# A graph layer in split precision: row sums turned by VectorE and sent through DRAM instead of turned by TensorE

## The chip, the cores and the metric

One core of one Trainium2 chip. The metric is the time of one execution in device microseconds. Three runs of the kernel before took 208.31, 208.48 and 209.1 us; the median is 208.48.

## What is computed

For each of 16 batches, with x of 512 nodes by 128 features and a sparse adjacency matrix adj of 512x512 (all float32):

```
h   = relu(layernorm(x))
HW_r = h @ W_r + c_r            (c_r: a row of 128 numbers, from W_edges and the last 16 rows of W_r), r = 0..6
A   = [adj, adj, shift, adj^T, adj^T, shift^T, identity]
out = x + max over r of (A_r @ HW_r) + b
```

Because A_r @ (h W_r + c_r) = (A_r h) W_r + rowsum(A_r) c_r, the kernel needs two aggregates per batch, g = adj h and gT = adj^T h, the row sums of adj and of its transpose, and seven products with W. (The shift matrices only move nodes around, and the maximum and the products are arranged so that r = 2, 5, 6 use h itself.)

## The kernel before

Everything is held transposed: 128 features on the partitions, 512 nodes along the free dimension. A batch is handled in these steps, and the engines work on neighbouring batches at the same time.

**Split precision.** From batch 2 on (`FIRST = 2`) each operand of a large matmul is split into a part that fits the fast float32r format and the rest: `a_hi` and `a_lo` for adj, `aT_hi` and `aT_lo` for its transpose, `h_hi` and `h_lo`, `hT_hi` and `hT_lo`, and so on. A product then takes three passes (hi·hi, lo·hi, hi·lo) of fast matmuls. adj has 4 chunks of 128 rows. ScalarE makes the hi parts (L414, L423), and as it copies it also adds up each row, which gives `sums`, 128 partitions by 2 directions by 4 chunks. The lo parts of chunks 0 and 1 are made by VectorE (L588, L595), those of chunks 2 and 3 by GpSimd (L330, L337). Batches 0 and 1 aren't split: their aggregates are plain float32 matmuls (L755, L762, L772, L781).

**TensorE, per batch.** `aggregate_T` (L791, L794, L800: 12 matmuls of 128x512), the turning of h (L733: 4 of 128x128), `aggregate` (L809, L811, L817: 12), `turn_sums` (L741: 4 of 128x128), the three products of h (L846, L847, L848: 9), `begin_products` (L836: four matmuls with only 32 rows, which add c_r times the row sum), and the other four products (12). `aggregate` waits until the last maximum of the batch before is taken, because product 6 and g share a PSUM bank. `begin_products` waits for the row sums (`sumsT`) and for `g_lo`.

**The row sums, before.** `part_sums` on GpSimd (L303 twice, L307 twice) writes the sums, split in hi and lo, into a mostly zero tile `sum_parts`; TensorE turns it by four matmuls with an identity (L741); ScalarE copies the result from PSUM into `sumsT` (L465). The rows 0 to 3 of each of four groups of 32 partitions are then used by L836.

**VectorE, per batch b**, in program order: statistics of x for batch b + 2 (L542, L549), `aT_lo` of b (L595), `gT_lo` (L611), `hT_lo` (L606), `rstd` and `shift` of b + 2 (L579, L581), `a_lo` of b + 1 (L588), `h_lo` of b + 1 (L601), `g_lo` of b (L616), then the running maximum `take_best`: two with an added column (L629) and four plain ones (L632), straight from the PSUM banks of the products.

**ScalarE, per batch b:** `a_hi` of b + 1, the standard deviation of b + 2, `gT_hi`, `hT_hi`, h and `h_hi` of b + 1, `g_hi`, the copy into `sumsT`, the first maximum (L472), `aT_hi` of b + 1.

**GpSimd, per batch b:** `finish` of b - 1 (L323, the output sum), then, once `h_lo` of b + 1 is made, the two splits of adj (L330), the DMA that adds x to the bias (L315), the two splits of the transpose (L337), `part_sums` of b + 1.

**Queues.** SP issues nearly all loads and stores, in an order written out by hand; each waits in place until its buffer is free: x of b + 3, adj of b + 2, store of b - 1, bias of b + 1, adjT of b + 2. GpSimd's own queue holds only the accumulating loads of x onto the bias.

There is no planner; each engine's program is the order in which its lines stand, and semaphores alone order the engines among each other.

Of the kernel before, what the change touches and what calls it, by code (L numbers as in the profile page):

```python
# [11 lines left out]
P = 128  # L12
# [14 lines left out]
FIRST = 2  # L27
NX = 4


def gnn_kernel(nc: bass.Bass, x: bass.AP, xT: bass.AP, adj: bass.AP, adjT: bass.AP, W: bass.AP,
               W_rel: bass.AP, W_edges: bass.AP, biasT: bass.AP, outT: bass.AP):
    B, N, F = x.shape
    R, FE, O = W.shape
    REL = FE - F
# [5 lines left out]
    x_dram = x.rearrange("b (c p) f -> b p c f", p=P)  # L41
    adj_dram = adj.rearrange("b (c p) m -> b p c m", p=P)
    adjT_dram = adjT.rearrange("b (c p) n -> b p c n", p=P)
    w_dram = W[:, :F, :].rearrange("r f o -> f r o")

    with ExitStack() as ctx:
# [37 lines left out]
        sumsT = sb("sumsT", [P, N], F32R)  # L84
# [94 lines left out]
        sumsT_ready = sem("sumsT_ready")  # L179
        hT_psum = sem("hT_psum")  # L180
# [31 lines left out]
        def _(sp):  # L212
            def load_x(b):
                q = b % NX
                if b >= NX:
                    sp.wait_ge(h_ready, b - NX + 1)
                    sp.wait_ge(h0_scaled, 1)
                sp.dma_start(x_sb[q][:, :, :], x_dram[b]).then_inc(x_in[q], 16)

            def load_adj(b):  # L220
                q = b % 2
                if b >= 2:
                    if b - 2 < FIRST:
                        sp.wait_ge(sums_ready, 2 * (b - 2) + 1)
                    sp.wait_ge(gT_psum, b - 1)
                if b >= 2 + FIRST:
                    sp.wait_ge(alo_ready, (b - 1 - FIRST) * ND)
                    sp.wait_ge(alo_last_ready, (b - 1 - FIRST) * NG)
                sp.dma_start(adj_sb[q][:, :, :], adj_dram[b]).then_inc(adj_in[q], 16)

            def load_adjT(b):
                q = b % 2
                if b >= 2:
                    if b - 2 < FIRST:
                        sp.wait_ge(sums_ready, 2 * (b - 2) + 2)
                    sp.wait_ge(g_psum, b - 1)
                if b >= 2 + FIRST:
                    sp.wait_ge(aTlo_ready, (b - 1 - FIRST) * ND)
                    sp.wait_ge(aTlo_last_ready, (b - 1 - FIRST) * NG)
                sp.dma_start(adjT_sb[q][:, :, :], adjT_dram[b]).then_inc(adjT_in[q], 16)  # L240
# [11 lines left out]
            sp.dma_start(x_sb[0][:, :HALF, :], x_dram[0][:, :HALF, :]).then_inc(x0_in[0], 16)  # L252
            for c in range(C):
                sp.dma_start(adj_sb[0][:, c, :], adj_dram[0][:, c, :]).then_inc(adj0_in[c], 16)
            sp.dma_start(w_edge[:, :], W_edges).then_inc(wrel_in, 16)
            sp.dma_start(w_rel[:, :], W_rel).then_inc(wrel_in, 16)
            for c in range(C):
                sp.dma_start(adjT_sb[0][:, c, :], adjT_dram[0][:, c, :]).then_inc(adjT0_in[c], 16)
                if c == 0:
                    sp.dma_start(w_sb[:, 0:1, :], w_dram[:, 2:3, :]).then_inc(wh_in, 16)  # L260
                    sp.dma_start(w_sb[:, 1:3, :], w_dram[:, 5:7, :]).then_inc(wh_in, 16)
                    load_x(1)
            sp.dma_start(w_sb[:, 3:5, :], w_dram[:, 3:5, :]).then_inc(wa_in, 16)
            sp.dma_start(w_sb[:, 5:7, :], w_dram[:, 0:2, :]).then_inc(wa_in, 16)
            load_adj(1)
            load_adjT(1)
# [3 lines left out]
            load_adj(2)  # L270
            load_adjT(2)
# [667 lines left out]
```

## Time and profile before

| what | value |
|---|---|
| median of three runs | 208.48 us |
| the profiled execution | 208.36 us |
| its span, from the first to the last instruction | 206.6 us |
| TensorE busy | 198.2 us, 96% |
| VectorE busy | 178.8 us, 87% |
| ScalarE busy | 162.3 us, 79% |
| GpSimd busy | 130.0 us, 63% |
| granted TensorE clock, mean | 1.000 |
| DMA: bytes moved, mean rate | 51.07 MB, 247 GB/s |
| packets in all / under 8 KB | 33747 / 33728 |

A busy share is the share of the span in which the engine works on something. Matmuls overlap in the pipeline, so a busy TensorE is not one at its peak; how long a group of matmuls holds the engine is read from the starts, or from the chain of waits. That chain is followed back from the last instruction: at each step to the operation that released it, or to the one before it on its engine. An operation of VectorE that doesn't wait for the one before it starts some 0.08 us before that one's recorded end.

### The profile page before, as it was taken

Reading aid. Unit: us, or ns where it says so; the run is one execution under the profiler, and the core shown is the slowest. Engines: PE = TensorE matmul, PEld = TensorE weight load, DVE = VectorE, ACT = ScalarE, POOL = GpSimd, SP = SyncE. Lnnn points to the kernel's source line nnn. Section 1 sums busy time; section 2 is a strip of 40 time slices with the busy share of each in tenths; the row PEclk is TensorE's granted clock in tenths of the full one; section 3 lists DMA queues with packets and bytes.
Section 4 is the critical chain, followed back from the end, with each engine's and each line's share of the span. In section 5 each row is a group of like instructions: output and inputs, shape, how many; then the busy total and the mean of one; then the engine's idle time right before and its main releaser. Section 6 shows DMA issues by size and latency. Waiting matters only on the chain.

```text
span 206.6 us, 3426 instructions
## 1 busy us (share of the span) xinstructions
PE 198.2 (96%) x922; PEld 152.2 (74%) x922; DVE 178.8 (87%) x411; ACT 162.3 (79%) x432; POOL 130.0 (63%) x166
## 2 busy tenths in 40 slices
PE   6999999799999999999999999999999999999991
PEld 6556468568788787878878787877878786887871
DVE  3587869999889998999889998999989999997565
ACT  3987989597979969696997969698896969685230
POOL 4140246969593977939594696919695486959600
PEclk9999999999999999999999999999999999999999
DMA  6999999987896959699795969779695969923201
GB/s 183 311 360 361 361 359 270 304 268 224 312 293 187 387 127 392 153 336 263 244 351 140 389 126 368 218 257 342 210 352 100 396 136 295 261 91 47 65 2 51
DMA packets 33747, 51.07 MB, mean 247 GB/s; under 512 B 1872, under 2 KB 11328, under 8 KB 33728
## 3 DMA queue, kind: packets, MB, share of 16 engines
q1 hardware_dynamic: 31152, 46.53, 66.2%
q0 software_dynamic: 2304, 4.20, 13.1%
q10 hardware_dynamic: 272, 0.13, 0.2%
q8 instruction: 7, 0.11, 0.2%
q14 instruction: 12, 0.10, 0.2%
HBM read 46.65 MB, written 4.19 MB: 246 GB/s over the span
## 4 chain that ended last, share of the span: by engine, by line
PE 70%; DMA 11%; DVE 6%; SPq 4%; POOL 3%; issue 3%; ACT 0%; DVEq 0%; ACTq 0%; POOLq 0%
PE bank_p L846 10%; PE bank_p L847 8%; PE bank_p L848 8%; DMA x_bias<-in_biasT_dram 8%; PE bank_g L809 5%; PE bank_g L811 5%; PE bank_g L817 5%; PE bank_gT L800 5%; PE bank_gT L794 5%; PE bank_gT L791 5%; DMA x_bias<-in_xT_dram 4%; PE bank_p L836 3%; PE bank_p L733 3%; PE bank_p L741 2%; DVE best L632 2%
## 5 line engine op out<-in xcount | busy, mean ns | idle before, releaser
L330 POOL TENSOR_TENSOR a_lo<-adj_sb,a_hi 128x512 fp32r<-128x512 f32 x28 | 36.1, 1310 | 38.0 <-DVE h_lo L601 36.9
L337 POOL TENSOR_TENSOR aT_lo<-adjT_sb,aT_hi 128x512 fp32r<-128x512 f32 x28 | 39.5, 1575 | 0.0
L632 DVE TENSOR_TENSOR best<-bank_p,best 128x512 f32<-128x512 f32 x48 | 33.2, 691 | 5.8 <-PE bank_p L848 4.7
L414 ACT ACTIVATE a_hi<-adj_sb 128x512 fp32r<-128x512 f32 x56 | 34.5, 620 | 0.0
L423 ACT ACTIVATE aT_hi<-adjT_sb 128x512 fp32r<-128x512 f32 x56 | 34.4, 620 | 0.0
L629 DVE SCALAR_TENSOR_TENSOR best<-bank_p,c_col,best 128x512 f32<-128x512 f32 x32 | 23.9, 748 | 5.0 <-ACT best L472 4.4
L595 DVE TENSOR_TENSOR aT_lo<-adjT_sb,aT_hi 128x512 fp32r<-128x512 f32 x28 | 25.4, 945 | 0.0
L435 ACT ACTIVATE h<-x_sb,shift,rstd 128x128 f32<-128x128 f32 x60 | 24.6, 488 | 0.0
L323 POOL TENSOR_TENSOR o_sb<-best,x_bias 128x512 f32<-128x512 f32 x15 | 20.8, 1384 | 3.4 <-DMA x_bias<-in_xT_dram 3.4
L846 PE MATMUL bank_p<-hT_hi,w_hi 128*128 128x512 f32 x48 | 20.1, 420 | 0.4 <-ACT sumsT L465 0.4
L588 DVE TENSOR_TENSOR a_lo<-adj_sb,a_hi 128x512 fp32r<-128x512 f32 x28 | 20.3, 765 | 0.0
L315 POOL DMA_DIRECT2D x_bias<-in_xT_dram x16 | 13.9, 868 | 9.2 <-DMA x_bias<-in_biasT_dram 9.2
L847 PE MATMUL bank_p<-hT_hi,w_lo 128*128 128x512 f32 x48 | 18.7, 390 | 0.0
L848 PE MATMUL bank_p<-hT_lo,w_hi 128*128 128x512 f32 x48 | 18.7, 389 | 0.0
L809 PE MATMUL bank_g<-aT_hi,h_hi 128*128 128x512 f32 x56 | 16.5, 416 | 1.5 <-DVE best L632 1.5
L387 ACT ACTIVATE std<-mean_var,eps 128x4 f32<-128x4 f32 x15 | 4.4, 296 | 16.7 <-DVE mean_var L549 16.7
L453 ACT ACTIVATE gT_hi<-bank_gT 128x512 fp32r<-128x512 f32 x16 | 9.5, 596 | 10.2 <-PE bank_gT L800 10.2
L303 POOL CAST sum_parts<-sums 128x16 fp32r<-128x16 f32 x32 | 14.8, 710 | 2.2 <-ACT summed L403 2.2
L817 PE MATMUL bank_g<-aT_lo,h_hi 128*128 128x512 f32 x56 | 15.3, 392 | 0.0
L811 PE MATMUL bank_g<-aT_hi,h_lo 128*128 128x512 f32 x56 | 15.1, 391 | 0.0
L800 PE MATMUL bank_gT<-a_lo,h_hi 128*128 128x512 f32 x56 | 15.0, 390 | 0.0
L791 PE MATMUL bank_gT<-a_hi,h_hi 128*128 128x512 f32 x56 | 15.0, 389 | 0.0
(118 smaller groups left out, 493.9 us busy)
## 6 DMA issues: line engine op xcount, KB each, us to landing
adj_sb<-in_adj_dram SPq DMA_DIRECT2D x15, 1024.0 KB, 5.5
adjT_sb<-in_adjT_dram SPq DMA_DIRECT2D x15, 1024.0 KB, 7.1
x_bias<-in_biasT_dram SPq DMA_DIRECT2D x16, 256.0 KB, 4.8
x_bias<-in_xT_dram POOLq DMA_DIRECT2D x16, 256.0 KB, 5.1
x_sb<-in_x_dram SPq DMA_DIRECT2D x15, 256.0 KB, 7.9
out_dram<-o_sb SPq DMA_DIRECT2D x15, 256.0 KB, 4.1
adj_sb<-in_adj_dram SPq DMA_DIRECT2D x4, 256.0 KB, 4.4
adjT_sb<-in_adjT_dram SPq DMA_DIRECT2D x4, 256.0 KB, 4.8
```

The source lines that it names most:

```text
L330: nc.gpsimd.tensor_tensor(a_lo[q][:, c, :], adj_sb[q][:, c, :], a_hi[q][:, c, :].bitcast(F32), ALU.subtract).then_inc(alo_last_ready, 1)
L337: nc.gpsimd.tensor_tensor(aT_lo[q][:, c, :], adjT_sb[q][:, c, :], aT_hi[q][:, c, :].bitcast(F32), ALU.subtract).then_inc(aTlo_last_ready, 1)
L414: nc.scalar.activation(a_hi[q][:, c, :], adj_sb[q][:, c, :], ACT.Copy, accum_out=sums[q][:, 0, c:c + 1]).then_inc(ahi_ready, 1)
L423: nc.scalar.activation(aT_hi[q][:, c, :], adjT_sb[q][:, c, :], ACT.Copy, accum_out=sums[q][:, 1, c:c + 1]).then_inc(aThi_ready, 1)
L595: nc.vector.tensor_tensor(aT_lo[q][:, c, :], adjT_sb[q][:, c, :], aT_hi[q][:, c, :].bitcast(F32), ALU.subtract).then_inc(aTlo_ready, 1)
L632: op = nc.vector.tensor_tensor(best[q][:, :], product, best[q][:, :], ALU.max)
L809: nc.tensor.matmul(bank_g[:, 0:N], h_hi[q][:, c, :], aT_hi[q][:, c, :], start=(c == 0), stop=False)
L811: nc.tensor.matmul(bank_g[:, 0:N], h_lo[q][:, c, :], aT_hi[q][:, c, :], start=False, stop=False)
L817: last = nc.tensor.matmul(bank_g[:, 0:N], h_hi[q][:, c, :], aT_lo[q][:, c, :], start=False, stop=(c == C - 1))
L846: nc.tensor.matmul(dst, w_hi[:, i, :], hi[:, nodes], start=start, stop=False)
L847: nc.tensor.matmul(dst, w_lo[:, i, :], hi[:, nodes], start=False, stop=False)
L848: return nc.tensor.matmul(dst, w_hi[:, i, :], lo[:, nodes], start=False, stop=stop)
```

## The change

1. **Row sums from batch 2 on (`TURNED = 2`).** GpSimd's `part_sums`, TensorE's L741 and ScalarE's L465 stay for batches 0 and 1 only. For the others VectorE copies the sums into a tile of 32 columns (hi), subtracts to get the lo columns, and transposes this tile in blocks of 32x32. SP stores the result to a scratch array in DRAM (128 runs of 128 bytes), waits for that, and issues four loads, each of which fills four partitions of `sumsT` with rows of 2 KB. `sumsT` becomes a pair. L836 waits for these loads.
2. **Place of the new work.** In VectorE's program it stands behind the third of the six maxima of the batch before.
3. **Batch 2 half whole.** Chunks 2 and 3 of its two aggregates are plain float32 matmuls; chunks 0 and 1 are still split. GpSimd no longer splits anything of batch 2.
4. **GpSimd's order.** `finish` waits for `aT_lo`, the splits for `a_lo` and `h_lo`; all four splits follow each other, and the DMA that adds x comes behind them.
5. **Queues.** adj and adjT from batch 3 on are loaded from ScalarE's queue, behind `hT_hi` and behind the first maximum; the standard deviation moves behind `hT_hi`.
6. **Layouts.** x, adj, adjT and W are laid out in DRAM by partitions, so that what a partition receives is one run.

```diff
+            def turn_blocks(b):
+                q = b % 2
+                i = b - TURNED + 1
+                s = sums[q][:, :, :].unsqueeze(2).to_broadcast([P, 2, 2, C])
+                dve.wait_ge(ahi_ready, (b - FIRST + 1) * NS)
+                dve.wait_ge(aThi_ready, (b - FIRST + 1) * NS)
+                nc.vector.tensor_copy(sum_cols[:, :, :, 0, :], s).then_inc(cols_hi, 1)
+                dve.wait_ge(cols_hi, i)
+                nc.vector.tensor_tensor(sum_cols[:, :, :, 1, :], s, sum_cols[:, :, :, 0, :].bitcast(F32),
+                                        ALU.subtract).then_inc(cols_lo, 1)
+                dve.wait_ge(cols_lo, i)
+                if i >= 2:
+                    dve.wait_ge(scratch_in, 16 * (i - 1))
+                nc.vector.transpose(sum_blocks[:, :], sum_cols[:, :, :, :, :].rearrange("p d k s c -> p (d k s c)")
+                                    .bitcast(F32)).then_inc(blocks_turned, 1)
...
                 for i in range(1, NPROD - int(b == B - 1)):
+                    if i == NH + 1 and b + 1 < B:
+                        turn_blocks(b + 1)
                     take_best(b, i)
...
+    scratch_blocks = scratch.rearrange("d r (c j s) -> j (d r c) s", c=C, s=GROUP)
+    scratch_rows = scratch.rearrange("d r n -> r d n").unsqueeze(2).to_broadcast([4, 2, 2, N])
...
+            def turn_sums(b):
+                i = b - TURNED + 1
+                q = b % 2
+                sp.wait_ge(blocks_turned, i)
+                sp.dma_start(scratch_blocks, sum_blocks[:, :]).then_inc(scratch_in, 16)
+                sp.wait_ge(scratch_in, 16 * i)
+                sp.wait_ge(prod_psum, (b - 1) * NPROD)
+                for r in range(4):
+                    sp.dma_start(sumsT[q][r:P:GROUP, :].bitcast(F32), scratch_rows[r]).then_inc(sumsT_in[q], 16)
...
             for b in range(1, B):
+                if b >= TURNED:
+                    turn_sums(b)
                 if b + 3 < B:
                     load_x(b + 3)
-                if b + 2 < B:
-                    load_adj(b + 2)
                 store(b - 1)
                 if b + 1 < B:
                     load_bias(b + 1)
-                if b + 2 < B:
-                    load_adjT(b + 2)
...
-            for b in range(1, B):
-                if b >= 2:
-                    finish(b - 1)
+            add_bias(2)
+            for b in range(2, B):
+                pool.wait_ge(aTlo_ready, (b - FIRST + 1) * ND)
+                finish(b - 1)
                 if b + 1 < B:
+                    pool.wait_ge(alo_ready, (b - FIRST + 2) * ND)
                     pool.wait_ge(hlo_ready, b - FIRST + 2)
                     split_adj_last(b + 1)
+                    split_adjT_last(b + 1)
                     add_bias(b + 1)
-                    split_adjT_last(b + 1)
-                    part_sums(b + 1)
...
+                split_gT(b)
+                split_hT(b)
                 if 2 <= b < B - 2:
                     std_of(b + 2)
-                split_gT(b)
-                split_hT(b)
+                if b + 2 < B:
+                    load_adj(b + 2)
                 if b + 1 < B:
                     make_h(b + 1)
                 split_g(b)
-                copy_sumsT(b)
+                if b < TURNED:
+                    copy_sumsT(b)
                 begin_best(b)
+                if b + 2 < B:
+                    load_adjT(b + 2)
...
+                if b == FIRST:
+                    pe.wait_ge(adj_in[q], times(b))
+                    for c in range(ND, C):
+                        nc.tensor.matmul(bank_gT[:, 0:N], h[q][:, c, :], adj_sb[q][:, c, :],
+                                         start=(c == ND), stop=False)
...
+                if b < TURNED:
+                    pe.wait_ge(sumsT_ready, b + 1)
+                else:
+                    pe.wait_ge(sumsT_in[b % 2], 64 * (b // 2))
...
-                turn_sums(b)
+                if b < TURNED:
+                    turn_sums(b)
```

## Rows read from the trace of the kernel before

**Rows 1.** Busy time by stretch, one batch: start:end, us, then busy us (x instructions).
```profile
115.17:127.00 11.83, 11.81 (x58) 9.36 (x58) 11.05 (x27) 10.09 (x28) 9.56 (x11) 1.00 0.87 278
```

**Rows 2.** The chain of waits (start us, us, what): L836 of batches 2 and 15, one batch between.
```profile
44.60 0.50 PE bank_p L836 x3
...
119.09 0.91 PE bank_gT L791 x4
...
125.02 0.39 PE bank_p L741 x4
125.41 0.29 PE bank_p L846
125.70 0.23 PE bank_p L847
...
127.51 0.43 PE bank_p L836 x3
...
130.94 0.91 PE bank_gT L791 x4
...
198.97 0.44 PE bank_p L836 x2
```

**Rows 3.** The timeline of VectorE and GpSimd, 111 to 128 us (start us, us, ...).
```profile
112.92 0.16 DVE L581 SCALAR_TENSOR_TENSOR shift<-mean_var,rstd 128x4 f32<-128x4 f32 x1
...
117.14 2.14 DVE L632 TENSOR_TENSOR best<-bank_p,best 128x512 f32<-128x512 f32 x3 [0.21 <-PE bank_p L848]
...
118.41 2.84 POOL L337 TENSOR_TENSOR aT_lo<-adjT_sb,aT_hi 128x512 fp32r<-128x512 f32 x2
...
121.12 1.29 DVE L595 TENSOR_TENSOR aT_lo<-adjT_sb,aT_hi 128x512 fp32r<-128x512 f32 x2
...
122.48 0.69 DVE L611 TENSOR_TENSOR gT_lo<-bank_gT,gT_hi 128x512 fp32r<-128x512 f32 x1
...
122.94 1.30 POOL L323 TENSOR_TENSOR o_sb<-best,x_bias 128x512 f32<-128x512 f32 x1
...
123.69 0.17 DVE L579 RECIPROCAL rstd<-std 128x4 f32<-128x4 f32 x1
123.89 0.37 DVE L581 SCALAR_TENSOR_TENSOR shift<-mean_var,rstd 128x4 f32<-128x4 f32 x1
...
125.38 0.68 DVE L601 TENSOR_TENSOR h_lo<-h,h_hi 128x512 fp32r<-128x512 f32 x1
...
126.14 2.54 POOL L330 TENSOR_TENSOR a_lo<-adj_sb,a_hi 128x512 fp32r<-128x512 f32 x2 [1.90 <-DVE h_lo L601]
...
126.95 1.54 DVE L629 SCALAR_TENSOR_TENSOR best<-bank_p,c_col,best 128x512 f32<-128x512 f32 x2 [0.29 <-ACT best L472]
```

**Rows 4.** The timeline at three meetings of VectorE and GpSimd.
```profile
13.40 0.74 POOL L360 TENSOR_TENSOR w_lo<-w_sb,w_hi 128x256 fp32r<-128x256 f32 x1 [2.98 <-DVE w_hi L665]
13.44 0.72 DVE L581 SCALAR_TENSOR_TENSOR shift<-mean_var,rstd 128x4 f32<-128x4 f32 x1
...
14.86 0.86 DVE L675 TENSOR_SCALAR c_low<-c_rest,row_lo 128x128 f32<-128x128 f32 x1
14.90 0.73 POOL L364 TENSOR_TENSOR w_lo<-w_sb,w_hi 128x256 fp32r<-128x256 f32 x1
...
31.23 1.28 POOL L330 TENSOR_TENSOR a_lo<-adj_sb,a_hi 128x512 fp32r<-128x512 f32 x1 [1.14 <-ACT a_hi L414]
31.28 1.79 DVE L588 TENSOR_TENSOR a_lo<-adj_sb,a_hi 128x512 fp32r<-128x512 f32 x1
```

**Rows 5.** DMA issues: what, queue, count, KB each, median us from issue to landing.
```profile
out_dram<-o_sb SPq DMA_DIRECT2D x15, 256.0 KB, 4.1
...
out_dram<-o_sb SPq DMA_DIRECT2D x2, 128.0 KB, 1.7
...
w_edge<-in_W_edges_dram SPq DMA_DIRECT2D x1, 0.4 KB, 3.5
```

**Rows 6.** The timeline of ScalarE's queue at its one load.
```profile
0.80 0.47 ACTq L475 DMA_DIRECT2D x_sb<-in_x_dram  x1
```

**Rows 7.** The timeline of TensorE: an unsplit aggregate, and aggregate of batch 2.
```profile
23.71 3.67 PE L781 MATMUL bank_g<-adjT_sb,h 128*128 128x512 f32 x8
...
37.89 1.19 PE L809 MATMUL bank_g<-aT_hi,h_hi 128*128 128x512 f32 x4 [1.45 <-DVE best L632]
```

More of the change, by code:

```diff
@@ L83, in gnn_kernel @@
         sum_parts = pair("sum_parts", [P, C, 2, 2, GROUP], F32R)
-        sumsT = sb("sumsT", [P, N], F32R)
+        sumsT = pair("sumsT", [P, N], F32R)
+        sum_cols = sb("sum_cols", [P, 2, 2, 2, C], F32R)
+        sum_blocks = sb("sum_blocks", [P, GROUP])
         x_bias = pair("x_bias", [P, N])
@@ L179, in gnn_kernel @@
         sumsT_ready = sem("sumsT_ready")
+        cols_hi = sem("cols_hi")
+        cols_lo = sem("cols_lo")
+        blocks_turned = sem("blocks_turned")
+        scratch_in = sem("scratch_in")
+        sumsT_in = [sem(f"sumsT_in{i}") for i in range(2)]
         hT_psum = sem("hT_psum")
@@ L697, in _ @@
                 take_best(1, i)
+            turn_blocks(2)
             for b in range(2, B):
@@ L783, in aggregate_whole, with split_chunks @@
                 last.then_inc(g_psum, 1)
+            def split_chunks(b):
+                return range(ND if b == FIRST else C)
             def aggregate_T(b):
@@ L806, in aggregate @@
                 pe.wait_ge(best_done, b * NBEST)
-                for c in range(C):
+                if b == FIRST:
+                    pe.wait_ge(adjT_in[q], times(b))
+                    for c in range(ND, C):
+                        nc.tensor.matmul(bank_g[:, 0:N], h[q][:, c, :], adjT_sb[q][:, c, :],
+                                         start=(c == ND), stop=False)
+                for c in split_chunks(b):
                     pe.wait_ge(aThi_ready, (b - FIRST) * NS + c + 1)
-                    nc.tensor.matmul(bank_g[:, 0:N], h_hi[q][:, c, :], aT_hi[q][:, c, :], start=(c == 0), stop=False)
-                for c in range(C):
+                    nc.tensor.matmul(bank_g[:, 0:N], h_hi[q][:, c, :], aT_hi[q][:, c, :],
+                                     start=(c == 0 and b > FIRST), stop=False)
+                for c in split_chunks(b):
                     nc.tensor.matmul(bank_g[:, 0:N], h_lo[q][:, c, :], aT_hi[q][:, c, :], start=False, stop=False)
-                for c in range(C):
+                for c in split_chunks(b):
                     if c < ND:
@@ L830, in begin_products, with add_sums @@
                     for nodes, to in zip(HALVES, last_banks):
-                        add_sums(NPROD - 1, to, nodes, start=True)
-            def add_sums(i, to, nodes=slice(0, N), start=False, stop=False):
+                        add_sums(b, NPROD - 1, to, nodes, start=True)
+            def add_sums(b, i, to, nodes=slice(0, N), start=False, stop=False):
                 group = ORDER_A.index(ORDER[i])
                 rows = slice(group * GROUP, (group + 1) * GROUP)
-                return nc.tensor.matmul(to[:, nodes], c_rows[rows, :], sumsT[rows, nodes], start=start, stop=stop)
+                return nc.tensor.matmul(to[:, nodes], c_rows[rows, :], sumsT[b % 2][rows, nodes], start=start, stop=stop)
             def passes(i, dst, nodes=slice(0, N), start=False, stop=False):
@@ L919, with by_partition @@
     batch, nodes, features = x.shape
+    chunks = nodes // P
+    def by_partition(a):
+        return np.ascontiguousarray(np.transpose(a.reshape(batch, chunks, P, a.shape[2]), (0, 2, 1, 3)))
     given = {
-        "x": np.ascontiguousarray(x),
+        "x": by_partition(x),
         "xT": np.ascontiguousarray(np.transpose(x, (0, 2, 1))),
-        "adj": np.ascontiguousarray(adj),
-        "adjT": np.ascontiguousarray(np.transpose(adj, (0, 2, 1))),
-        "W": np.ascontiguousarray(L0_gnn_W),
+        "adj": by_partition(adj),
+        "adjT": by_partition(np.transpose(adj, (0, 2, 1))),
+        "W": np.ascontiguousarray(np.transpose(L0_gnn_W[list(ORDER), :features, :], (1, 0, 2))),
         "W_rel": np.ascontiguousarray(L0_gnn_W[:, features:, :]).reshape(-1, L0_gnn_W.shape[2]),
```

127 lines of the change are left out of this document (62 added, 65 removed).

## Prediction

> **What bounds the kernel now.** I began with busy time by stretch, one stretch per batch: in a steady batch of 11.83 us TensorE is busy for 11.81, VectorE 11.05, ScalarE 10.09, GpSimd 9.56, at a granted clock of 1.00, which is the 2.4 GHz level [rows 1]. Two engines are nearly full, so I read the chain of waits next. From L836 of batch 2 at 44.60 to L836 of batch 15 at 198.97 the chain lies almost wholly on TensorE [rows 2]: 154.4 us for 13 batches, 11.87 each. TensorE paces the kernel. One batch runs from 119.09 to 130.94, 11.85 us, of which the turning of the row sums (L741) holds 0.39, and the first matmul behind it needs 0.29 where the ones that follow need 0.23 [rows 2].
>
> Then VectorE's timeline, because the change gives it work. Its three maxima start at 117.14, and 0.29 us before 126.95 it has finished everything up to the next batch's first two maxima: 9.52 us [rows 3]. With those two (1.54) and the join it needs 11.0 a batch. In that stand two waits that are not work: the shift took 0.37 instead of 0.16, and gT_lo started some 0.15 late behind aT_lo (122.48, though aT_lo was over at 122.41 and two such operations otherwise overlap by 0.08) [rows 3]. Bare VectorE work is **10.7 us a batch**, against TensorE's 11.85.
>
> Last I looked for operations that took longer than their like. VectorE's split of 128x512 needs 0.68 (two in 1.29 [rows 3]), but took 1.79 when GpSimd had begun its own split 0.05 us earlier; the shift of 128x4 took 0.72 when a GpSimd subtract had begun 0.04 earlier, and ended as that one ended; a VectorE operation with one tensor input (c_low) took 0.86 beside a GpSimd subtract of 0.73 [rows 4]. So a VectorE operation that reads two SBUF tensors stands still until a GpSimd operation in progress ends, however small it is. This decides the case.
>
> **The change part by part.** *TensorE.* L741 goes from batch 2 on: 0.39, and 0.06 of the slow first matmul, so 0.45 a batch; 11.85 becomes 11.4. Nothing else of its steady work changes.
>
> *VectorE.* Each batch gains a copy of 16 elements, a subtract of 16 and a block transpose of 32, each waiting for the one before. The nearest row is the reciprocal and the shift that waits for it: starts 0.20 apart [rows 3]. Three make 0.6; the transpose isn't in the trace, so 0.45 (ends of 0.15 each, the bare duration) to 0.8 (a transpose twice as long). 10.7 + 0.6 = 11.3, just under the new 11.4: **no slack is left**, and any wait of VectorE above 0.1 us a batch is paid in full. In return the finish now waits for aT_lo, so GpSimd's output sum runs beside gT_lo and hT_lo, which read PSUM; that takes away the waits named above, which I have already left out of the 10.7.
>
> *Where the new operations fall.* GpSimd starts its splits of the next batch 0.08 after h_lo ends (126.06, 126.14), two in 2.54 [rows 3]. Until now the bias DMA stood between them and the two splits of aT; it is moved behind, so the first aT split follows at about 2.6 after h_lo, the second at about 3.85, the end at about 5.1 (1.25 to 1.4 each, from two in 2.84 [rows 3]). VectorE reaches turn_blocks after g_lo (0.6), two maxima (1.54) and the third (0.71): about 2.75 after h_lo. That is in the middle of those splits. If VectorE came later it would not escape: turn_blocks waits for the last aT_hi of ScalarE, and GpSimd's splits need these same operands, so they start when it does or shortly before. The subtract reads two SBUF tensors; by rows 4 it waits for the split in progress. The copy comes within 0.15 us of the start of the first split and can be just before or just behind it.
>
> I take **one wait of about 1.05 us** a batch (most of one split of 1.25, as the subtract asks 0.2 after the split began). Ends: 0.3, when it meets a split at its end, and 1.4, a whole long one. So VectorE sets the pace: 10.7 + 0.6 + 1.05 = 12.35 us a batch, 0.5 slower than now, and TensorE waits for the maxima, g_lo and hT_lo.
>
> *The way through DRAM.* The blocks go out in 128-byte runs, the queue's engine waits, then four loads are issued. The trace shows no such transfer. Nearest: a load of 0.4 KB in pieces of 4 bytes landed after 3.5 us in a full stretch, 128 KB at the quiet end after 1.7 [rows 5]; four issues at 0.47 each, ScalarE's row [rows 6]. So 1.7 + 1.7 + 1.9 = 5.3 to 3.5 + 3.5 + 1.9 = 8.9; I take 7. What covers it: from the turned blocks (third maximum over at 117.85, plus 0.6) to L836 of the next batch (127.51 less 0.45) are 8.6 us [rows 2, 3]. Cost nothing; if the cover is gone, the excess is paid per batch. By the Trainium skill ("DMA: Bandwidth & Descriptors", "Anatomy of one DMA — SWDGE (gpsimd) path") a transfer costs about 2.0 us fixed, most of it the receipt; its fit is for GpSimd's queue. By that the way would take an estimated 5.9 and batch 2 would not wait for it at all; the row of 3.5 is longer, and the measurement counts.
>
> *Batch 2 (half whole).* GpSimd splits nothing of it, so VectorE's a_lo at 31.28 no longer meets it: two splits at 1.79 become 1.29, the maxima of batch 1 end 2.2 us sooner, and TensorE's wait of 1.45 at 37.89 goes [rows 7]. L741 goes too (0.45). Against that four chunks run in full precision: eight such matmuls, four chunks, took 3.67 [rows 7], 0.9 a chunk, against three passes at 0.23; 0.2 each, +0.8. L836 of batch 2 would come at 44.60 - 1.1 = 43.5. But its sums start only when batch 1's maxima are over, about 37.89 - 2.2 = 35.7, and need 0.6 and the way through DRAM: 41.6 to 45.2. I take 44.0.
>
> *The rest.* ScalarE loses a copy of 0.6 and issues two DMAs at 0.47 [rows 6]: +0.3, 10.4 a batch, hidden behind 11.4 and more; its waits before these loads are all met by work it has just waited for. Without that cover the aT_hi splits, and turn_blocks, come 0.3 later. SP now waits for the blocks ahead of an x load, a store and a bias load. These blocks are turned in the batch before, ahead of the finish for which the store already waits, and x has three batches of lead: nothing. GpSimd loses the four small operations for the sums and sits idle in their place. The layout by partitions makes runs longer; in the first 33 us TensorE waits for chunks of adj, but eight matmuls there take hardly longer than the 3.67 of batch 1 [rows 7]: nothing, between 0 and -1 us.
>
> **The sum.** To L836 of batch 2: 44.0. Twelve batches at 12.35: 148.2. The one before the last has no statistics (about 1.2 less on VectorE), so TensorE's 11.4. From L836 of batch 15 to the end 206.6 - 198.97 = 7.6 [rows 2]. Outside the span the profiled execution spends 208.36 - 206.6 = 1.8. Together 213.0 against 208.36; the median of the runs is 208.48, 0.1 above it. **Forecast 213.0**, slower by 2.2%. Its own range, with 0.45 to 0.8 for the work and 0.3 to 1.4 for the wait, and 43.5 to 45 for batch 2: 202 (never below TensorE's 11.4) to 220, most of it 207 to 217.
>
> **Rivals.** *No collision (faster).* If these operations are too short to be held, or GpSimd is off the port when they come, TensorE stays the bound: 44.0 + 13 x 11.4 + 7.6 + 1.8 = 201.6. The place is turn_blocks, the price is the wait there, and it decides below 0.7 us a batch: at a period of 12.0 the sum is 208.8. For it: a reciprocal beside GpSimd's output sum (122.94 to 124.24) took 0.17 [rows 3]. Against it: the shift, smaller still, waited.
>
> *Two waits.* If the copy too is held, it waits for the first split and the subtract for the second, as GpSimd takes its next operation in between: 2.15 us instead of 1.05, 13.45 a batch: 44.0 + 12 x 13.45 + 11.95 + 7.6 + 1.8 = 226.7. For it: c_low with one tensor input waited [rows 4]. Against it: the copy may come first, and no plain copy beside GpSimd is in the trace. The Trainium skill ("SBUF — State Buffer", "Who interferes with whom") has copies, casts and tensor_scalar in their two-port modes take the pair shared with GpSimd, and whoever is first holds it for the whole instruction; by that rule this is the outcome unless the copy is first, and c_low's 0.86 agrees with it.
>
> *The way through DRAM is late.* If each leg takes 4.1, as stores of 256 KB in mid-run do [rows 5], it needs 10.1 instead of 8.6, and TensorE waits 1.5 us a batch at L836 whatever VectorE does: 44.0 + 13 x 12.9 + 9.4 = 221. Against it: these transfers are 16 KB, and no load stands ahead of them in their queue.
>
> **How the numbers follow.** Chances: one wait 0.37, no collision 0.33, two waits 0.22, late sums 0.08. The range reaches from no collision less 1.5 for the layout and a good batch 2, 200.0, to 224.0, which leaves out most of the two-wait case. A measurement of this kernel tells 0.5%, about 1 us. Faster: no collision and the low end of one wait, 0.36; within 0.5%: 0.06; slower 0.58.
>
> **What would show it.** Right: L741 gone from batch 2 on; in the steady part VectorE without idle time, its subtract in turn_blocks at 1 us or more and ending when a GpSimd aT split ends, TensorE idle at L836 or L846 with VectorE as releaser, a period near 12.35. A subtract of 0.2 and TensorE unbroken at 11.4 would make it wrong towards faster; copy and subtract both above 1 us towards 227; TensorE waiting at L836 for sumsT's loads would show the late sums.

## The result and the profile after

The changed kernel takes **226.53 us** (median of four runs, 224.19 to 227.72) against 208.39 us for the kernel before on the same chip: a ratio of 1.083, with a 95% interval of 1.075 to 1.092. (The ratio leaves out the run of 227.72, which lies more than 1.5% above the fastest; with it the medians alone give 1.087.) It is 18 us slower; the forecast was 213.0, and its range ended at 224.0. The profiled execution took 225.96, with a span of 224.2.

Busy time by engine, and the granted clock in 40 slices of the span, from the page of the kernel after:

```profile
PE 201.0 (90%) x862; PEld 146.9 (66%) x862; DVE 189.5 (85%) x453; ACT 155.6 (69%) x418; POOL 104.2 (46%) x106
...
PEclk9999999958999999999999999999996999999998
```

No engine is full any more. TensorE is busy for nearly as long as before, but its 201.0 now holds stretches at a lower clock, and the span is 18 us longer.

From its waits (engine, line, what was waited for: us in all, times, longest):

```profile
PEld bank_p L897 <- DMA sumsT<-scratch_dram: 18.7, 12, 3.1
DVE best L671 <- PE bank_p L909: 14.8, 15, 3.5
PE bank_p L897 <- DMA sumsT<-scratch_dram: 13.1, 9, 2.7
```

TensorE waits at L897 (L836 before) for the row sums in most batches, and VectorE waits 14.8 us for product 3, which follows L897. The chain of waits through one batch, L897 at 100.52 to L897 at 114.35, as far as it runs through the sums (start us, us, what):

```profile
102.64 0.29 DVE sum_cols L648
...
102.96 1.23 DVE sum_cols L650
...
104.21 0.22 DVE sum_blocks L655
...
104.45 2.00 DMA scratch_dram<-sum_blocks
...
106.47 0.51 SPq L237
...
108.06 6.25 DMA sumsT<-scratch_dram
...
114.35 0.50 PE bank_p L897 x3
```

Where TensorE's own work stood in the chain of before [rows 2], there is now the store to DRAM (2.00), three issues (1.6 with their gaps), and the fourth load from its issue until all four have landed (6.25). The same turning in VectorE's and GpSimd's timeline, with the first turning of the kernel, at 36.79, ahead of it:

```profile
36.79 0.16 DVE L648 CAST sum_cols<-sums 128x16 fp32r<-128x16 f32 x1
36.98 0.18 DVE L650 TENSOR_TENSOR sum_cols<-sums,sum_cols 128x16 fp32r<-128x16 f32 x1
37.20 0.21 DVE L655 STREAM_TRANSPOSE sum_blocks<-sum_cols 128x32 f32<-128x32 f32 x1
...
101.60 2.54 POOL L328 TENSOR_TENSOR aT_lo<-adjT_sb,aT_hi 128x512 fp32r<-128x512 f32 x2
...
102.64 0.28 DVE L648 CAST sum_cols<-sums 128x16 fp32r<-128x16 f32 x1
...
102.96 1.22 DVE L650 TENSOR_TENSOR sum_cols<-sums,sum_cols 128x16 fp32r<-128x16 f32 x1
```

At 36.79 no GpSimd operation runs beside them, and copy and subtract take 0.16 and 0.18. In the steady part (batches 4 to 15) the subtract took 1.21 to 1.23 in nine batches of twelve and 0.18 in three, the copy 0.25 to 1.29: on average the two waited **1.38 us** a batch.

From here on the **period** is the distance between the starts of that first matmul of `begin_products` in batches 2 and 15, over 13: 11.87 before, **13.11** after. It splits in two without a rest: 4.11 from L897 to the issue of the next batch's store, and 9.00 from that issue to the next L897, "the way" below. The way is not all DRAM: the four loads had landed 8.4 us after the store's issue on average (5.5 to 9.9), and in batches 3, 8 and 12 they had landed 0.5 to 5.0 us before TensorE came to L897. In the profiled executions the difference of 17.6 us is 1.5 for batch 2 (L897 at 46.06 for L836 at 44.60 [rows 2]), 13 x 1.24 = 16.1 for the period, and next to nothing in the tail. Two of the 13 batches are long without late sums of their own: the one from 46.06 took 14.25 and the one from 166.74 took 12.95, at granted clocks of 0.78 and 0.87.

### The profile page after: what moved, and what is told of

The parts are those of the page before. It is cut to its first block, busy times and chain, and to the rows that moved or that the text cites. A ratio compares the mean times of both kernels' runs of the same rounds, so it can differ in the third digit from the quotient of the medians.

```text
span 224.2 us, 3374 instructions
## 1 busy us (share of the span) xinstructions
PE 201.0 (90%) x862; PEld 146.9 (66%) x862; DVE 189.5 (85%) x453; ACT 155.6 (69%) x418; POOL 104.2 (46%) x106
## 3 DMA queue, kind: packets, MB, share of 16 engines
q0 software_dynamic: 2304, 4.20, 12.9%
HBM read 47.11 MB, written 4.42 MB: 230 GB/s over the span
## 4 chain that ended last, share of the span: by engine, by line
DMA 32%; PE 30%; DVE 17%; SPq 8%; ACT 6%; issue 6%; ACTq 1%; DVEq 0%
DMA sumsT<-scratch_dram 16%; DMA scratch_dram<-sum_blocks 10%; SPq L237 5%; PE bank_p L907 5%; DVE sum_cols L650 4%; PE bank_p L909 4%; PE bank_p L908 4%; DVE sum_cols L648 3%; DMA adj_sb<-in_adj_dram 3%; DMA w_sb<-in_W_dram 3%; PE bank_p L897 3%; DVE best L671 3%; ACT a_hi L410 2%; ACT aT_hi L419 2%; PE bank_gT L842 2%
## 5 line engine op out<-in xcount | busy, mean ns | idle before, releaser
L321 POOL TENSOR_TENSOR a_lo<-adj_sb,a_hi 128x512 fp32r<-128x512 f32 x26 | 32.9, 1285 | 27.8 <-DVE a_lo L611 27.8
L671 DVE TENSOR_TENSOR best<-bank_p,best 128x512 f32<-128x512 f32 x48 | 32.6, 680 | 15.5 <-PE bank_p L909 14.8
L314 POOL TENSOR_TENSOR o_sb<-best,x_bias 128x512 f32<-128x512 f32 x15 | 19.2, 1283 | 38.4 <-DVE aT_lo L618 35.9
L328 POOL TENSOR_TENSOR aT_lo<-adjT_sb,aT_hi 128x512 fp32r<-128x512 f32 x26 | 33.1, 1297 | 0.0
L897 PE MATMUL bank_p<-sumsT,c_rows 32*128 32x512 f32 (+1 forms) x49 | 8.3, 505 | 13.7 <-DMA sumsT<-scratch_dram 13.1
L611 DVE TENSOR_TENSOR a_lo<-adj_sb,a_hi 128x512 fp32r<-128x512 f32 x28 | 18.1, 688 | 0.0
L618 DVE TENSOR_TENSOR aT_lo<-adjT_sb,aT_hi 128x512 fp32r<-128x512 f32 x28 | 17.7, 673 | 0.0
L897 PEld LDWEIGHTS bank_p<-sumsT,c_rows 32*128 32x128 f32 x49 | 3.3, 188 | 20.1 <-DMA sumsT<-scratch_dram 18.7
L875 PE MATMUL bank_g<-aT_lo,h_hi 128*128 128x512 f32 x54 | 15.8, 401 | 0.1
L907 PE MATMUL bank_p<-gT_hi,w_hi 128*128 128x512 f32 x32 | 14.7, 459 | 0.0
```

The source lines that it names most:

```text
L314: nc.gpsimd.tensor_tensor(o_sb[q][:, :], best[q][:, :], x_bias[q][:, :], ALU.add).then_inc(out_ready, 1)
L321: nc.gpsimd.tensor_tensor(a_lo[q][:, c, :], adj_sb[q][:, c, :], a_hi[q][:, c, :].bitcast(F32), ALU.subtract).then_inc(alo_last_ready, 1)
L328: nc.gpsimd.tensor_tensor(aT_lo[q][:, c, :], adjT_sb[q][:, c, :], aT_hi[q][:, c, :].bitcast(F32), ALU.subtract).then_inc(aTlo_last_ready, 1)
L671: op = nc.vector.tensor_tensor(best[q][:, :], product, best[q][:, :], ALU.max)
L907: nc.tensor.matmul(dst, w_hi[:, i, :], hi[:, nodes], start=start, stop=False)
```

## The experiments

The theory to begin with: a closed loop. L897, product 3, the third maximum, the turning with its waits for GpSimd, the store and the loads, and L897 of the next batch follow one another, so both delays are paid in series. Rival A: the port waits alone cost the time. Rival B: the late sums alone do.

**1. GpSimd out of the way.** GpSimd's aT splits wait for the turned blocks:

```diff
             def split_adjT_last(b):
+                pool.wait_ge(blocks_turned, b - TURNED + 1)
```

> GpSimd starts its two splits of aT of a batch only once that batch's blocks are turned, so the copy and the subtract of the row sums meet no GpSimd operation and should take 0.16 and 0.18 us, as they do in the changed kernel where GpSimd rests. Theory (a closed loop: product 3, its maximum, the turning, the way through DRAM, begin_products of the next batch): the loop loses about 1.35 us a batch (copy 0.76, subtract 0.93 on average) but keeps the 9.2 us of the way through DRAM: period 11.9 instead of 13.1, time about 210 (208 to 213), and TensorE still waits for the row sums in every batch. Rival A (the port waits alone cost the time, VectorE sets the pace): period 11.4, time 202. Rival B (the late sums alone cost it, the port waits only fill idle time of VectorE): unchanged, 224 to 227.

Measured: 222.09 us, period 12.64; copy and subtract 0.16 to 0.18 in every batch. The part from L897 to the store fell from 4.11 to 3.02, but the way grew from 9.00 to 9.62. The transfers themselves did not: the sums landed 8.3 us after the store's issue on average, as before, but spread from 6.6 to 11.5. All three forecasts, the theory's and both rivals', missed. Busy time by stretch, in batches of three kinds (us, then PE, PEld, DVE, ACT, POOL busy, the clock, DMA share, GB/s):

```profile
48.29:62.52 14.23, 14.23 (x54) 10.95 (x55) 9.91 (x27) 5.11 (x13) 5.42 (x5) 0.78 0.48 141
...
101.17:112.53 11.36, 11.36 (x54) 8.95 (x54) 10.56 (x29) 9.45 (x28) 7.20 (x7) 1.00 0.76 242
136.55:150.31 13.76, 11.40 (x54) 8.95 (x53) 13.05 (x30) 11.77 (x34) 8.80 (x8) 0.99 0.89 288
```

Where the sums landed in less than 8.6 and the clock was full, the batch ran at TensorE's own 11.36, and 2.77 + 8.6 is just that; what lands sooner gains nothing. In four batches like the third line they landed after 9.9 to 11.5 and the excess was paid in full, 9.2 of the 16.6 us that the 13 batches took beyond 11.36 each. The other 7.4 are in four batches like the first line (12.8 to 14.2): their own sums had landed after 6.6 to 7.0, but each stands behind a batch whose sums TensorE had awaited for 2.4 to 5.0 us, and TensorE ran them at a clock of 0.78 or 0.87.

**2. The way through DRAM out of the loop.** `begin_products` takes the sums of the batch before, from three buffers (so the output lacks its own batch's sums; the store also waits for the loads of the batch before):

```diff
-                q = b % 2
+                q = b % 3
...
-                    pe.wait_ge(sumsT_in[b % 2], 64 * (b // 2))
+                    pe.wait_ge(sumsT_in[(b - 1) % 3], 64 * ((b - 3) // 3 + 1))
```

> Here begin_products adds the row sums of the batch before instead of its own, from the same stores and loads into three buffers: the way through DRAM has a whole batch more and cannot delay TensorE, while the copy and the subtract can still meet GpSimd's splits. The output then holds the wrong batch's row sums. Theory (loop): without the way through DRAM the port waits alone are left, VectorE's 10.7 + 0.6 + about 1.35 = 12.65 us a batch: period 12.3 to 12.8, batch 2 no longer waits (begin_products near 43.5 instead of 46.1), time 211 to 220. Rival A (the port waits alone cost the time): period unchanged at 13.1, time 222 to 226. Rival B (the late sums alone): TensorE is the bound again, period 11.4, time about 202.

Measured: 221.87 us, period 12.93 (13.13 in the steady batches), and no wait for sums. This misses the theory's range on the high side and lies by rival A's. One batch in VectorE's and GpSimd's timeline:

```profile
109.28 2.54 POOL L327 TENSOR_TENSOR a_lo<-adj_sb,a_hi 128x512 fp32r<-128x512 f32 x2 [2.05 <-DVE a_lo L618]
...
111.77 2.55 POOL L334 TENSOR_TENSOR aT_lo<-adjT_sb,aT_hi 128x512 fp32r<-128x512 f32 x2
...
112.00 1.10 DVE L655 CAST sum_cols<-sums 128x16 fp32r<-128x16 f32 x1
...
113.14 1.21 DVE L657 TENSOR_TENSOR sum_cols<-sums,sum_cols 128x16 fp32r<-128x16 f32 x1
```

The copy waits for one split and the subtract for the next, in 12 of the 14 turnings: two waits, 1.97 us. By the page, the chain is now mostly VectorE's:

```profile
DVE 62%; PE 16%; issue 12%; DMA 3%; ACT 3%; SPq 2%; DVEq 0%; ACTq 0%
```

Each cause alone keeps the kernel near 222. So there are **two bounds at nearly the same height**: the loop (13.11 a batch as changed, 12.64 with the port free, both with some batches at a lower clock) and VectorE held at the port (13.13). Taking one away uncovers the other.

**3. Both edits together.**

> Both edits of the two runs before together: no GpSimd split beside the turning, and the row sums of the batch before in begin_products (the output holds the wrong batch's row sums). Theory: nothing is left but TensorE's own work, 11.4 us a batch, and VectorE's 11.3 beside it: about 43.5 + 13 x 11.4 + 7.7 + 1.8 = 201 (200 to 204). If a third thing costs time as well (the adj loads that are now issued late, or VectorE's 11.3 not fitting into 11.4), it is seen here alone: 205 or more.

Measured: 206.35 us, period 11.74. Of the 20 us, the two single edits gave 4 and 5. (These are single runs, and the kernel after itself ranged over 3.5 us.) The rest over 201 is the third thing that was allowed for: five of the 13 batches took 11.9 to 12.9, the others 11.3 to 11.5. In one of the long ones the timeline shows VectorE's a_lo beside GpSimd's output sum, 2.67 for the two splits instead of 1.28; in the other four it is the small `shift` that stands still beside the same sum, 0.86 to 1.87 instead of 0.17:

```profile
87.78 0.86 POOL L312 DMA_DIRECT2D x_bias<-in_xT_dram  x1 [3.09 <-DMA x_bias<-in_biasT_dram]
...
87.86 2.67 DVE L619 TENSOR_TENSOR a_lo<-adj_sb,a_hi 128x512 fp32r<-128x512 f32 x2
...
88.39 1.58 POOL L320 TENSOR_TENSOR o_sb<-best,x_bias 128x512 f32<-128x512 f32 x1
```

**4. The rest of the change alone.** TensorE turns all row sums again:

```diff
-TURNED = 2
+TURNED = 16
...
                     split_adjT_last(b + 1)
+                    part_sums(b + 1)
                     add_bias(b + 1)
...
-            turn_blocks(2)
...
-                    if i == NH + 1 and b + 1 < B:
-                        turn_blocks(b + 1)
```

> The changed kernel with the row sums of all batches turned as before the change: small operations of GpSimd, four matmuls of TensorE, a copy by ScalarE. Half of the third batch in full precision, the order of GpSimd, the queues and the layouts stay as changed. Theory: all of the loss lies in the turning, so this runs at the period before, 11.85, or slightly under it, and gains the 1.1 us of batch 2: 207 (204 to 209). Rival C (the queues, GpSimd's order or the layouts cost something too): above 210.

> The changed kernel with TensorE turning the row sums of all batches, once more, now timed against the kernel before in several rounds. One look gave 205.8 with batch 2's begin_products 1.9 us earlier and a period of 11.81 instead of 11.87. Theory: 205.5 to 206.5, a ratio near 0.988. Rival (that difference was the chance of one look): a ratio of 0.995 to 1.005.

Measured: 205.8 in a single run; in the repetition a median of 206.55 (12 runs) against 208.81 (17 runs), ratio **0.989**, interval 0.986 to 0.993. The other parts together are a gain of about 1%, and this version beats both kernels. In the single run `begin_products` of batch 2 stands at 42.74 (43.34 in the repetition, 44.60 before), the period is 11.81, and the page has the chain on TensorE again:

```profile
PE 96%; DVE 2%; issue 0%; POOL 0%; DVEq 0%; POOLq 0%
```

**5. Another place for the turning.** One maximum earlier, ahead of that of product 3; without and with GpSimd's splits held until the blocks are turned:

```diff
-                    if i == NH + 1 and b + 1 < B:
+                    if i == NH and b + 1 < B:
                         turn_blocks(b + 1)
...
                 sp.wait_ge(blocks_turned, i)
+                if i >= 2:
+                    sp.wait_ge(sumsT_in[(b - 1) % 2], 64 * ((b - 1) // 2))
```
```diff
+                    pool.wait_ge(blocks_turned, b + 2 - TURNED)
                     split_adj_last(b + 1)
```

> The turning stands one maximum earlier in VectorE's program, ahead of the maximum of product 3 instead of behind it. Product 3 is the first that needs the row sums, so the turning of the next batch no longer follows begin_products of this one: the loop is cut in its place. SP's store now waits for the loads of the batch before (it shares the scratch array). GpSimd is left as it is, so the copy and the subtract still meet its splits. Theory: as with the wrong batch's sums, VectorE with its port waits sets the pace (12.9 a batch there), some batches still wait for sums: 218 to 223. Rival (what counts is the sum of all delays before the store, wherever the turning stands): unchanged, 224 to 227.

> The earlier place of the run beside it, and GpSimd starts all four splits of a batch only once its blocks are turned. Theory: the loop is cut and the copy and the subtract meet nothing (0.16, 0.18); the way through DRAM gets 2.8 us more cover, so it is hidden up to about 11 us. TensorE is then the bound, as with both causes taken away (206.4, where GpSimd's output sum met VectorE's split in some batches): 202 to 207, under the kernel before. Rival (the way through DRAM still ends last): TensorE waits for the row sums and it stays above 208.

Measured: 220.58 for the first, a single run, as expected (period 12.70, copy 0.59 and subtract 1.15 on average). The second missed: a median of 223.14 of four runs, 219.51 to 225.59, where 202 to 207 was expected; on this chip the kernel before itself ranged from 207.99 to 213.07. Copy and subtract were bare there (0.16 to 0.18), but an earlier store is not an earlier landing. In its chain:

```profile
123.59 4.42 DMA scratch_dram<-sum_blocks
```

The store that took 2.00 in the kernel after took 4.42, and L897 came 10.2 to 14.2 us after the store's issue in batches 3 to 14; the sums had landed after 6.3 to 14.2, and TensorE waited 13.7 us for them in all. An adjT load issued by ScalarE 3.8 us ahead (119.83, store at 123.59) is in flight beside the store and lands 4.1 us after its issue; in the kernel after it was issued 6.3 us ahead (98.11, 104.45) and landed 1.7 us after. It need not be adjT's load that holds the store: a bias load of 256 KB in SP's own queue, issued 4.2 us ahead, lands 4.3 us after, and in experiment 1 a store with adjT's load alone beside it for 3.3 us (65.28) took 2.16. The edit has a price of its own, too: GpSimd's a_lo waited 60.7 us for the turned blocks. So the question is what the way consists of.

**6. How long the way is by itself.** Edit 1, with SP waiting for the sums to land, so that its x load marks the landing, and with adj and adjT loads of a quarter:

```diff
                     turn_sums(b)
+                    sp.wait_ge(sumsT_in[b % 2], 64 * (b // 2))
...
-                act.dma_start(adj_sb[q][:, :, :], adj[b])
+                act.dma_start(adj_sb[q][:, 0, :], adj[b][:, 0, :])
...
-                act.dma_start(adjT_sb[q][:, :, :], adjT[b])
+                act.dma_start(adjT_sb[q][:, 0, :], adjT[b][:, 0, :])
```

> GpSimd's splits of aT wait for the turned blocks (as in the first experiment), and the loads of adj and adjT from batch 4 on, or as far as ScalarE issues them, fetch one chunk of four: 256 KB instead of 1 MB each, so that the output uses stale chunks. SP also waits for the row sums to land before it issues the x load, so that this issue marks the landing. Theory (the way through DRAM is long because its small loads share the DMA engines with an adj load of 1 MB issued while they are): from the issue of the store to the landing it takes 5.4 to 6.5 us instead of 8.6 to 11.5; TensorE doesn't wait for sums and the time is 200 to 204. Rival (the two legs and four issues have this length by themselves): 8.6 us or more also here, and TensorE still waits in the steady part.

> The same with whole loads of adj and adjT, the control for the run beside it: only SP's wait for the landing is added to the first experiment. From the issue of the store to the landing 8.3 to 11.2 us by both theories, and about 222 us, a little more where SP's wait holds up the loads behind it.

One way of the control, with whole loads, in the timeline:

```profile
99.27 0.60 SPq L232 DMA_DIRECT2D scratch_dram<-sum_blocks  x1
...
102.66 2.08 SPq L237 DMA_DIRECT2D sumsT<-scratch_dram  x4
...
103.38 0.34 ACTq L481 DMA_DIRECT2D adj_sb<-in_adj_dram  x1
...
110.35 0.33 SPq L225 DMA_DIRECT2D x_sb<-in_x_dram  x1
```

And one with quarter loads:

```profile
104.66 0.59 SPq L232 DMA_DIRECT2D scratch_dram<-sum_blocks  x1
...
106.67 2.05 SPq L237 DMA_DIRECT2D sumsT<-scratch_dram  x4
...
111.58 0.33 SPq L225 DMA_DIRECT2D x_sb<-in_x_dram  x1
```

From the store's issue to the x load that marks the landing it takes 9.1 us on average with whole loads (6.8 to 11.9), and the kernel 223.04; with quarter loads 7.0 (6.5 to 7.7) and **202.07**, period 11.35. The landing is a little above the 5.4 to 6.5 that I expected; the time is as expected. So some 2 us of this stretch, and most of its spread, come from the large loads in flight beside it. The quarter loads relieve everything else that waits for a DMA too, so the 21 us are not the way's alone.

**7. Large loads moved in the queues.** With edit 1, adj and adjT go back to SP's queue, behind the row sums (first run); or only adj does (second); or only adj, and GpSimd issues the x-to-bias DMA behind the output sum (third):

```diff
                     load_x(b + 3)
+                if b + 2 < B:
+                    load_adj(b + 2)
                 store(b - 1)
                 if b + 1 < B:
                     load_bias(b + 1)
+                if b + 2 < B:
+                    load_adjT(b + 2)
```
```diff
                 finish(b - 1)
+                add_bias(b)
...
                     split_adjT_last(b + 1)
-                    add_bias(b + 1)
```

> GpSimd's splits of aT wait for the turned blocks, as in the first experiment (222.1), and adj and adjT from batch 3 on are loaded from SP's queue again, in the order from before the change: adj behind the four loads of the row sums and the x load, adjT behind the store of the output and the load of the bias. Theory (the adj load of 1 MB, issued on another queue while the four loads are, is what stretches them): with it behind them in one queue the way through DRAM ends 8.6 us after its store is issued in nearly every batch, the period falls from 12.6 to 11.4 to 11.9 and the time to 204 to 212. Rival (it is the amount in flight, whichever queue it came from, above all adjT's load ahead of the store): 220 or more, the store's own landing at 4 us and longer.

> GpSimd's splits of aT wait for the turned blocks, and only adj goes back to SP's queue, behind the four loads of the row sums and the x load; adjT stays on ScalarE's queue, where it is issued some 6 us before the store of the next sums. Theory (the two legs are each stretched by the 1 MB load in flight beside them: with adj behind them the loads took 3.4 to 3.9 us from the first issue instead of 6.5 to 7, and with adjT on ScalarE's queue the store 2.0 instead of 4 to 6.9): the whole way takes 5.4 to 7 us, TensorE doesn't wait for sums, and the time is that of both causes taken away, 203 to 208. Rival (the loads' time comes back in another place, as a_hi waiting for an adj that is issued later): 210 or more, ScalarE waiting for adj by over 2 us a batch.

> The kernel beside it with one more edit: GpSimd issues the DMA that adds x to the bias behind the output sum of the batch before instead of ahead of it, so that a late load of the bias no longer holds up the output sum and pushes it beside VectorE's a_lo, as in the batches that took over 12 us with both causes taken away (a_lo twice in 2.67 there instead of 1.28). Theory: periods of 11.35 to 11.5 in every batch, 201 to 204. Rival (that meeting has another cause, or the DMA issue now delays the splits): no better than the kernel beside it.

Measured: 211.0 (a single run), 223.72 (ratio 1.069, 1.062 to 1.077) and 226.17 (1.083, 1.076 to 1.090). The chain of the first through one way:

```profile
106.94 6.51 DMA scratch_dram<-sum_blocks
...
113.47 0.51 SPq L237
...
115.05 1.76 DMA sumsT<-scratch_dram
...
116.85 0.49 PE bank_p L898
```

Against the kernel after, the legs have changed places: there 2.00 and 6.25, here **6.51 and 1.76**. The leg that runs beside a freshly issued 1 MB load is the long one: the loads are short now that adj's is behind them, and the store is long, as adjT's load was issued 2.1 us ahead of it in the same queue and landed 7.2 us after the store's issue. (An adj load, the output's store and a bias load were in flight too, and landed within 3.7.) Theory and rival each had one leg right. The way is hardly shorter on average than in experiment 1 (9.4 for 9.62), but steadier, the clock stays at 1.00, and the period is 12.19.

The second run was to have both short legs and is a miss; its rival describes it:

```profile
ACT a_hi L425 <- DMA adj_sb<-in_adj_dram: 39.0, 12, 6.7
```

SP waits in place for its store, so adj's load behind it was issued late and flew together with adjT's, and a_hi waited 39.0 us for it. That wait alone does not set the time: in the first run, which took 211.0, it was 34.6. In the second run the stores met two 1 MB loads in many batches and took up to 6.3 us; TensorE's matmuls waited for the sums in two batches and for g_lo in seven, so which of these costs how much is not shown. In the third run the wait of the x-to-bias DMA is gone from the long waits, but the sums still land 5.4 to 12.7 us after the store's issue and the batches take 11.3 to 15.5, so whether that edit helps by itself stays open.

## Why the prediction was wrong, step by step

**What bounds the kernel now** was read rightly: VectorE had no slack, and a small VectorE operation with two SBUF inputs stands still until GpSimd's operation ends (the subtract: 1.22 at 102.96, over 0.04 us after the split).

**TensorE 11.4 a batch:** right, 11.36 in undisturbed batches and 11.35 where nothing stands in its way. The rival "no collision" was priced at 201.6; the run with quarter loads and a free port took 202.07.

**VectorE's new work, 0.6:** right, 36.79 to 37.41 for the three.

**One wait of 1.05:** the size was near (1.38 on average), but it is a mixture: the subtract waited in nine batches of twelve and the copy in most. Where VectorE sets the pace (experiment 2) both wait, 1.97, at 13.13 a batch and 221.87, close to the rival "two waits" (13.45, 226.7). The step that failed is "the copy may come first": a split was already in progress when it came, as the splits follow each other without a gap. The prediction took 2.75 us from h_lo to the turning; in the trace of before h_lo ends at 114.88 and the third maximum at 117.85, 2.97 later, because VectorE waits 0.21 for product 3 [rows 3]. That is behind the start of the first aT split, at about 2.6. By the rule of the Trainium skill that the prediction weighed ("SBUF — State Buffer", "Who interferes with whom") the copy waits unless it is first; the trace agrees, 1.10 for a cast of 16 elements that bare takes 0.16. The prediction's own example fits the rule less well: c_low waited, though its recorded start (14.86) lies before that of GpSimd's subtract (14.90) [rows 4].

**The way through DRAM, 7 us, "cost nothing":** this is the step that failed most. The sums landed 8.4 us after the store's issue on average, and later than the cover of 8.6, at 9.1 to 9.9, in seven of the 13 batches. The argument "these transfers are 16 KB, and no load stands ahead of them in their queue" looked at one queue, and did not hold there either: SP's bias load, issued at 97.87, was in flight until 1.5 us after the store of 104.45. An adj load of 1 MB from ScalarE's queue beside the four loads stretched them to 6.25. A smaller transfer can hold the store: the four long stores of the kernel after (3.6 to 4.0, batches 4, 13, 14 and 15) each stand 0.4 us behind GpSimd's DMA of 256 KB that adds x to the bias, in the last of them with no adj or adjT load in flight (GpSimd's timeline, then the chain):

```profile
208.88 0.86 POOL L306 DMA_DIRECT2D x_bias<-in_xT_dram  x1
```
```profile
209.24 3.88 DMA scratch_dram<-sum_blocks
```

The Trainium skill's fixed 2.0 us a transfer ("DMA: Bandwidth & Descriptors", "Anatomy of one DMA — SWDGE (gpsimd) path"), a fit for GpSimd's queue, agrees with a store that has nothing beside it, 1.99 and 2.00 (52.03 and 204.02 in experiment 1), and not with the same store at 6.51. The rival "late" had put 10.1 and 221 on it, with a chance of 0.08; the port freed and the way left in place gave 222.09. That the two times lie so close is in part luck: 7.4 us of it are batches at a lower clock, which the rival had not priced.

**Treating the cases as alternatives:** the cover of 8.6 was measured from the end of the third maximum plus 0.6 of bare work. The wait at the port lies in just that stretch, and so takes from the cover what it costs. In the prediction's own terms, 8.6 less 1.05 leaves 7.55 at a period of 11.4, less than the upper end of the way, 8.9; the sum for that, 2.8 + 1.05 + 8.9 = 12.75 a batch, was never made (2.8 is 11.4 less 8.6). Measured it is 4.11 + 9.00 = 13.11. The waits at the port and the late sums, priced as alternatives, both came true; because they lie at the same height the time is 226.5 and not their sum, and neither could be removed alone.

**Batch 2 at 44.0:** it came at 46.06. Half whole was right: where its sums are turned by TensorE it comes at 42.74 and 43.34 (43.5 predicted, with L741 gone). But its turning began at 36.79, not 35.7, and the way took 8.6; TensorE waited 2.71 for the sums, and the batch after it ran at a clock of 0.78 and took 14.25, a cost that no step had:

```profile
46.06:60.31 14.25, 14.25 (x54) 10.96 (x54) 9.92 (x27) 6.65 (x19) 5.03 (x5) 0.78 0.68 205
```

**The rest:** the other parts, costed at nothing, together with batch 2 are the gain of 1% of experiment 4. The layout by partitions brought nothing at the start: `begin_products` of batch 0 stands at 19.85 after and at 19.38 in the single run of experiment 4, 19.11 before. The output sum does run clear of aT_lo now, as predicted (aT_lo 107.55 to 108.81, the sum from 108.91). SP's queue was costed at nothing too: that holds while the loop decides, but with both causes gone the bias loads, which stand behind SP's wait in place, are what the long batches of experiment 3 begin with.

**Size:** for the sum of 213.0 the trace has 46.06 + 13 x 13.11 + 7.7 + 1.8 = 226.0. Of the 13, 2.1 are batch 2 and 10.8 the period. (In the rival "two waits" the 11.95 for the batch before the last does not follow from its terms, 13.45 less 1.2 = 12.25; it is 0.3 us.)

**Open:** how the way would do with one load instead of four, some 1.5 us of issues less, was not tried.

## What to carry to other kernels

When a step is taken off a full engine and sent by a longer way, draw the loop that it closes from batch to batch and add all that lies in it: a wait and a late transfer in the same loop are not alternatives, and a cover is to be counted after the waits that come ahead of it. Cost a small transfer by what every queue, its own included, has in flight at that moment, and not by its size. And when removing one cause gives little, remove both before dropping either: here 4 us, 5 us, and 20.

## What the runs showed of the hardware that was not expected

A 16 KB store took 2.00 us from issue to landing by itself. Beside larger transfers it depends on which and when. With a 1 MB load of ScalarE's queue in flight for another 1.7 or 3.3 us it took 2.00 and 2.16; with such a load and a 256 KB load of its own queue in flight for over 4 us, 4.42; with the 1 MB load in its own queue, 1.3 to 2.7 us ahead (first run of experiment 7), 5.1 to 6.9. Behind a 256 KB accumulating DMA of GpSimd, issued 0.4 us ahead, it took 3.6 to 4.0. The last of four 8 KB loads landed 1.76 us after its issue with the 1 MB load behind it, and 6.25 with that load issued beside it.

A TensorE wait of a few microseconds can cost more than itself. The chain of the last run of experiment 7 shows it behind a wait of 4.1 us for sums:

```profile
121.39 5.28 DMA sumsT<-scratch_dram
...
126.71 0.80 PE bank_p L897 x2
...
128.24 0.43 PE bank_p L908
...
130.46 0.23 PE bank_p L908
```

For some 3.2 us after the wait the same matmul takes 0.43 instead of 0.23, and `begin_products` 0.80 instead of 0.43: the granted clock, 1.00 before the wait, is 0.51 from 126.71 to 130.00, so it has gone from its level of 2.4 GHz to that of 1.2. Four batches of experiment 1 lost their clock in this way. The length of the wait alone does not decide it: the clock fell behind a wait of 1.62 in the kernel after (at 166.74), and it stayed at 1.00 behind one of 2.66 in the first run of experiment 5 (at 46.06). In experiment 3, in the single run of experiment 4 and with quarter loads it stayed at 1.00 throughout the steady part.
